# Decoder layer on one core: batch 0's keys and values projected in the turn before, x1's transposes earlier, and another spread of the first turn's score blocks

## The reference, cut to what matters

```
# 1: a lookup: the 8 best of 8192 keys for each token, and their values
h      = scan(h @ A + x @ Bm);  importance = softmax(x . (h @ W_imp.T))
shared = sum over n of neuron_w[b, n] * compress[n]            # a 256 x 128 matrix for each batch
scores = (x @ shared) @ K.T / sqrt(128)                        # 256 x 8192 for each batch
x1     = layernorm(x + sum of softmax(top8(scores)) * V[top8 index])
# 2: cross attention, 16 heads of 64, keys and values from the context
q = x1 @ Wq;  k, v = split(ctx @ Wkv)
attn   = softmax(clip(mask(q k / 8), -5, 5))
x2     = layernorm(x1 + (attn v) @ Wo + bo)
# 3: each expert set picks one token of each group of 32
x3     = layernorm(x2 + permuted feed-forward(x2))
```

## Time and profile before

| | before |
|---|---|
| median of 3 runs | 1438.27 us |
| lowest, highest | 1435.86, 1443.63 us |
| the profiled execution | 1435.45 us, its span 1433.4 us |
| busy over the span | PE 92%, PEld 69%, DVE 76%, ACT 50%, POOL 50% |
| mean granted TensorE clock | 0.964 of full speed |

### The profile page before, as it was taken

The page is one execution under the profiler, slowest core; times in us unless marked ns, Lnnn a source line. Parts: engine busy times, 40 slices in busy tenths (PEclk is TensorE's granted clock), DMA queues, the critical chain, the costliest instruction groups (busy, mean ns, idle before and its releaser), DMA issues.

```text
span 1433.4 us, 25145 instructions
## 1 busy us (share of the span) xinstructions
PE 1320.5 (92%) x9781; PEld 993.1 (69%) x9781; DVE 1087.0 (76%) x1625; ACT 723.9 (50%) x1361; POOL 723.2 (50%) x1010
## 2 busy tenths in 40 slices
PE   9765799999999999999999999999999969568998
PEld 5453577777878686868686878777777747346765
DVE  1369999888888888897978888888888841147567
ACT  1353465556464646465655555555556433135455
POOL 0524455556565646574746574655556573330225
PEclk7877899999999999999999999999999999889999
DMA  9451212121212222221213131212121210162323
GB/s 373 161 175 48 66 45 71 52 71 53 71 53 74 64 70 65 63 71 56 81 43 93 46 84 48 75 52 71 41 72 41 70 53 23 30 225 83 105 68 126
DMA packets 63174, 115.88 MB, mean 81 GB/s; under 512 B 9936, under 2 KB 43728, under 8 KB 61904
## 3 DMA queue, kind: packets, MB, share of 16 engines
q1 hardware_dynamic: 45968, 67.68, 15.6%
q0 software_dynamic: 14848, 41.96, 10.0%
q10 hardware_dynamic: 2240, 4.63, 0.9%
HBM read 103.49 MB, written 10.75 MB: 80 GB/s over the span
## 4 chain that ended last, share of the span: by engine, by line
PE 82%; DVE 9%; issue 3%; POOL 2%; DMA 2%; ACT 1%; SPq 0%; POOLq 0%; DVEq 0%; ACTq 0%
PE proj_bank L369 39%; PE score_bank L369 30%; PE sim_bank L369 10%; DVE cand_val L1048 2%; DVE cand_idx L1049 2%; PE score_bank L705 2%; DVE x_sum L1072 2%; POOL exp L1277 1%; POOL v_rows L1248 1%; DMA sc_in<-shared_compress 1%; PE sim_bank L705 1%; DVE dispatchedT L1187 1%; PE sim_bank L639 1%; DMA x_pair<-x_scratch 0%; PE sim_bank L520 0%
## 5 line engine op out<-in xcount | busy, mean ns | idle before, releaser
L811 ACT COPY score_row<-score_bank 128x512 f32<-128x512 f32 x512 | 298.6, 588 | 173.9 <-PE score_bank L369 102.2
L1048 DVE MAX8 cand_val<-score_row 128x8 f32<-128x2048 f32 x128 | 292.2, 2283 | 105.1 <-ACT score_row L811 105.1
L1248 POOL DMA_INDIRECT v_rows<-in_V,top_idx x256 | 248.2, 969 | 188.2 <-DVE top_idx L1062 106.3
L1277 POOL TENSOR_SCALAR exp<-exp,exp_bound 128x256 f32<-128x256 f32 x512 | 241.8, 488 | 107.0 <-ACT exp L823 106.3
L1049 DVE FIND_INDEX8 cand_idx<-cand_val,score_row 128x8 uint32<-128x2048 f32 x128 | 292.5, 2285 | 0.0
L369 PE MATMUL score_bank<-keysT_hi,qT_hi 128*128 128x512 f32 x512 | 219.1, 428 | 31.0 <-ACT score_row L811 30.0
L369 PE MATMUL score_bank<-keysT_lo,qT_hi 128*128 128x512 f32 x512 | 205.3, 401 | 0.0
L369 PE MATMUL score_bank<-keysT_hi,qT_lo 128*128 128x512 f32 x512 | 205.0, 400 | 0.0
L823 ACT ACTIVATE exp<-sim_bank 128x512 f32<-128x512 f32 x256 | 139.0, 595 | 91.8 <-PE sim_bank L369 91.8
L369 PE MATMUL sim_bank<-qT_heads,kT 64*128 64x256 f32 x1024 | 145.2, 402 | 7.7 <-ACT exp L823 7.7
L369 PEld LDWEIGHTS score_bank<-keysT_hi,qT_hi 128*128 128x128 f32 x512 | 98.2, 192 | 69.8 <-ACT score_row L811 34.9
(11 more groups left out here) (184 smaller groups left out, 2258.7 us busy)
## 6 DMA issues: line engine op xcount, KB each, us to landing
kT<-den_scratch SPq DMA_DIRECT2D x64, 256.0 KB, 4.0
x_pair<-x_scratch SPq DMA_DIRECT2D x32, 256.0 KB, 2.8
f_quads<-in_f POOLq DMA_DIRECT2D x32, 256.0 KB, 5.8
comp_then_wqkv_raw<-in_comp SPq DMA_DIRECT2D x6, 1024.0 KB, 18.3
xT_by_step<-in_xTs SPq DMA_DIRECT2D x4, 1024.0 KB, 9.1
keysT_raw<-in_KmT ACTq DMA_DIRECT2D x8, 512.0 KB, 12.7
xT_in<-in_xT SPq DMA_DIRECT2D x16, 256.0 KB, 3.8
x_sum<-in_x SPq DMA_DIRECT2D x32, 128.0 KB, 2.1
```

The source lines that it names most:

```text
L811: nc.scalar.copy(srow[n // PER % 2][:, i * CB:(i + 1) * CB], scb[n % 3]).then_inc(sem("score_evac"), 1)
L1048: own(nc.vector.max(cv[:, tile, cs], srow[g % 2][:, :]))
L1248: pool.indirect_dma_start(out=vg[:, k, :], out_offset=None, in_=V_rows, in_offset=bass.IndirectOffsetOnAxis(ap=i8[:, tile, k:k + 1], axis=0))\
L1277: last = nc.gpsimd.tensor_scalar(ex[i % NEX][:, k, :], ex[i % NEX][:, k, :], ub[:, k, c:c + 1], E_LO, ALU.min, ALU.max)
```

## The change

In turn -1 the keys and the values of batch 0 (`K` 0 to 3, then `V` 0 to 3) are projected two at a time at the end of each couple, behind its four blocks; before, the values stood beside b28 to b31 of that turn, and the keys beside b0 to b3 of turn 0. ACT's copies move with them. The rounding of the context of batch 0 to `ctx_hi` goes to the head of turn -1 on ACT; its counterpart `ctx_lo` on POOL stays where it was.

The transposes of batch 0's x1 (PE), their copies `x1T_hi` (ACT) and `x1T_lo` (DVE) go ahead of the last row of turn -1.

In turn 0 the blocks are spread anew by a function `blocks(c)`, which gives how many stand in the first part, beside the queries, in each couple and beside the values. Turn 0 has none in the first part, one beside each query job, six in each couple, one beside each value job; all other turns are as before. `den_inverse(0, 0)` goes from behind row 4 to ahead of row 3, and the weights of tile 1 of batch 1 (`weights8`) on ACT go behind couple 1.

```diff
+        def blocks(c):
+            if c == 0:
+                return [0, 0], [1, 1, 1, 1], [6, 6, 6, 6], [1, 1, 1, 1]
+            return [4, 4], [1, 1, 1, 1], [4, 4, 4, 4], [1, 1, 1, 1]
...
@@ PE
                 for j in range(4):
-                    if cross:
+                    if cross and c > 0:
                         project(("K", c, j), 1, 2 * j * P, cth, ctl)
-                    score(c, j)
+                    if early[0]:
+                        score(c, next(place))
...
-                    for e in range(4):
-                        score(c, 12 + 4 * j + e)
+                    for _ in range(couple[j]):
+                        score(c, next(place))
+                    if c == -1:
+                        need(pe, "ctx_lo", 1)
+                        need(pe, "w_lo", len(WCHUNKS))
+                        for i in (2 * j, 2 * j + 1):
+                            if i < 4:
+                                project(("K", 0, i), 1, 2 * i * P, cth, ctl)
+                            else:
+                                project_value(0, i - 4)
                 if cross:
                     values(c, NP // 2 - 1)
                     denominators(c, 1)
-                if mid:
+                if c == -1:
+                    x1_transpose(0, 0)
+                    x1_transpose(0, 1)
+                if mid and m:
                     need(pe, "ctx_lo", m + 1)
...
@@ DVE
+                if c == 0:
+                    den_inverse(c, 0)
                 candidates(c, 3)
...
                 candidates(c, 4)
-                if cross:
+                if cross and c > 0:
                     den_inverse(c, 0)
...
+                if c == -1:
+                    x1_lo(0, 0)
+                    x1_lo(0, 1)
                 candidates(c, 6)
                 candidates(c, 7)
-                if mid:
+                if mid and m:
                     x1_lo(m, 0)
                     x1_lo(m, 1)
```

More of the change, by code:

```diff
@@ L71, in turn_jobs @@
         jobs += [("q", c + 3, 0)]
+    if c == -1:
+        jobs += [("K", 0, j) for j in range(4)]
     if cross:
@@ L574, in _ @@
                 cross, mid, prep, out = (0 <= b < B for b in (c, m, a + 1, p))
+                early, query, couple, value = blocks(c)
+                place = iter(range(2 * SCORES))
                 if cross:
@@ L590, in _ @@
                         last.then_inc(full(key), 1)
-                    score(c, 4 + 2 * tile)
-                    score(c, 5 + 2 * tile)
+                    for _ in range(early[1] // 2):
+                        score(c, next(place))
                 if cross:
@@ L599, in _ @@
                         project(("Q", c, j), 0, 2 * j * P, x1h, x1l)
-                    score(c, 8 + j)
+                    for _ in range(query[j]):
+                        score(c, next(place))
                 if prep:
@@ L615, in _ @@
                     denominators(c, 1)
-                if mid:
+                if c == -1:
+                    x1_transpose(0, 0)
+                    x1_transpose(0, 1)
+                if mid and m:
                     need(pe, "ctx_lo", m + 1)
-                    need(pe, "w_lo", len(WCHUNKS))
                 for j in range(4):
-                    if mid:
[L621 to L629, removed]
+                    if mid and m:
+                        project_value(m, j)
+                    for _ in range(value[j]):
+                        score(c, next(place))
+                if mid and m:
                     x1_transpose(m, 0)
@@ L832, in _ @@
                 cross, mid, prep = (0 <= b < B for b in (c, m, a + 1))
+                early, query, couple, value = blocks(c)
+                place = iter(range(2 * SCORES))
+                if c == -1:
+                    context_hi(0)
                 for j in range(4):
-                    if cross:
+                    if cross and c > 0:
                         need(act, "ot_done", 2 * (c - 1) + 1 + j // 2)
                         heads_out(("K", c, j), kt[:, 2 * j:2 * j + 2, :].rearrange("p a s -> p (a s)"))
-                    score_out(c, j)
-                for e in range(4, 8):
-                    score_out(c, e)
+                    if early[0]:
+                        score_out(c, next(place))
+                for _ in range(early[1]):
+                    score_out(c, next(place))
                 for j in range(4):
@@ L844, in _ @@
                         heads_out(("Q", c, j), qt[:, 2 * j:2 * j + 2, :].rearrange("p a s -> p (a s)"))
-                    score_out(c, 8 + j)
-                    if mid and j == 1:
+                    for _ in range(query[j]):
+                        score_out(c, next(place))
+                    if mid and c and j == 1:
                         weights8(m, 1)
@@ L857, in _ @@
                         exps(c, 2 * j + 1)
-                    for e in range(4):
-                        score_out(c, 12 + 4 * j + e)
+                    for _ in range(couple[j]):
+                        score_out(c, next(place))
+                    if c == -1:
+                        for i in (2 * j, 2 * j + 1):
+                            if i < 4:
+                                heads_out(("K", 0, i), kt[:, 2 * i:2 * i + 2, :].rearrange("p a s -> p (a s)"))
+                            else:
+                                value_out(0, i - 4)
                     if c == -2 and j < 3:
```

38 lines of the change are left out of this document (29 added, 9 removed).

## The result

The changed kernel took 1458.79 us (median of four runs, 1453.89 to 1459.24) against 1438.17 us for the kernel before in the same comparison. The ratio is 1.0129, with a 95% interval of 1.0106 to 1.0151. The profiled execution took 1458.98 us, its span is 1456.9 us, 23.5 us over the one before. Of all the executions behind this document one, of a kernel in experiment 8, fell in a slow state (3175.62 us) and is left out of its ratio.

The account below looks back on a forecast made before the run. From turn 1 on PE sets the pace, so the time PE ends turn 0 decides. +2.5 + 9.8 + 2.5 = +14.8 us on the profiled 1435.45 gives 1450.2; forecast 1451 us, 8 in 10 range 1440 to 1457.

Parts of the forecast that it names:

- wrong in size: Sign: size is wrong if less than 38 or more than 46 us lie between the first `values` and turn 1.
- What bounds the kernel: From turn 1 PE sets the pace at 68.5 us a turn; any shift of turn 1's start moves the end equally.
- Turn -1: Key jobs wait some 5.7 us for `ctx_lo`, then run at half clock; DVE starts turn 0 2.5 us later.
- Up to the first values: In turn 0 PE arrives near 192 and waits for POOL's clips until about 207.4, through with first `values` at 208.5.
- Behind the first values: Rest of turn 0 takes 42.6 us against 32.8 before: +9.8, of which 4.3 are six blocks and 5.5 waits.
- 5.5 of waits: Waits between PE and DVE in turn 0 behind the first `values`, 5.5 of the +9.8 us.
- 2.5 for the clock: After PE's long wait ahead of the first `values`, work at half speed costs 2.5 us, between 0 and 3.1.
- the one behind the value sum of tile 1: Late turn 0: row 4 4.6 us, copies of b24 and b27 1.3, last `values` and denominators 3.7, V jobs and transposes 8.9.
- only the six blocks count: Second rival: the chain's waits are hidden and only order counts; +2.4 to +6.8 us, 1438 to 1445, chance 0.18.
- Faster: Third rival: PE finds the clips done at the first `values`; down to -8 us, 1430 us, chance 0.06.
- The fourth, more lost: Rival: second clock fall at the wait for row 6, or norm at 4.7 us; +19 to +23, 1455 to 1461, chance 0.09.
- the port as a loss: DVE's norm, sharing a port with POOL, takes 0.4 us if POOL's clips are through; otherwise the sum is 4.3 higher.

Follow-up runs that it names:

- experiment 8: Changed kernel with POOL's turn 0 order changed, then also `ctx_lo` of batch 0 early, then also the first reciprocal behind row 3: 1.0021, 0.9996, 0.9964 of the kernel before.
- the other trace of the changed kernel: The changed kernel measured once more with nothing altered: 1.0133 of the kernel before.
- experiment 5: Changed kernel with POOL making `ctx_lo` of batch 0 ahead of its gathers in turn -1: 1.0108 of the kernel before.
- experiment 6: Changed kernel with turn 0's old block spread, the reciprocal back behind row 4, and `ctx_lo` of batch 0 ahead of POOL's gathers: 0.9983 of the kernel before.
- experiment 4: Changed kernel with POOL making tile 1's inverse deviation behind the last head instead of head 9 in turn 0: 1.0120 of the kernel before.
- experiment 3: Changed kernel with POOL clipping heads 0 to 3 ahead of the gathers in turn 0: 1.0099 of the kernel before.
- last version of experiment 8: Changed kernel with POOL's turn 0 order changed, `ctx_lo` of batch 0 early and the first reciprocal behind row 3: 1437.02 us against 1441.69, ratio 0.9964.

## Why the prediction was right, and where its size was off

The forecast was 1451 us, with 1440 to 1457 for 8 in 10. The median of 1458.79 us lies 1.8 us above that; the ratio, applied to the 1438.27 us that the forecast started from, gives 1456.8, just inside. The prediction called itself wrong in size if less than 38 or more than 46 us lay between the first `values` and turn 1; there were 51.4, so by this sign its size was wrong. What follows goes through its steps.

**What bounds the kernel.** Right. The shift at PE's start of turn 1 is 263.10 - 238.76 = 24.3 us, and the span grew by 23.5. Of these, 2.3 us lie ahead of the changed part and are a difference between two executions; 22.0 us are the change's in this trace, and 18.5 in the other trace of the changed kernel, which is nearer to the ratio.

**Turn -1.** Right step by step. The first key job waits 5.60 us for `ctx_lo` (forecast 5.7) and runs at 0.50. DVE waits 1.14 us for row 4 (forecast 1.4) and 3.1 us in two pieces for the transposes (3.1). The start of turn 0 on DVE is 2.6 us later, forecast 2.5. That this cost goes away with an early `ctx_lo` is what experiments 5, 6 and 8 add.

**Up to the first values.** Right: PE came to them at 196.06 (forecast near 192, 2.3 us of the difference being the later trace) and waited 10.85 and 0.91 us for clips behind gathers behind `merge`. The point came 25.8 us after D where it was 24.9 before; the 0.9 us are the second half of `values` at half clock.

**Behind the first values.** Here the size was off. The forecast was 37.1 us of work, 5.5 of waits and 2.5 for the clock, 45.1 in all. Measured were 51.4 us in one execution of the changed kernel and 48.6 in the other (the stretch of the other, columns as in rows 1):

```profile
211.37:259.92 48.55, 39.65 (x248) 26.90 (x247) 34.22 (x41) 22.79 (x44) 23.23 (x36) 0.92 0.21 54
```

PE is idle for 8.9 us in both. So the term that was too small in both is the waits, 8.9 us where the sum had 5.5. The rest differs between the executions: PE is busy for 42.5 us at a mean clock of 0.86 in the one, 39.7 us at 0.92 in the other. Against 37.1 us of work that is, as an estimate, 5.4 and 2.6 us for the clock.

The step that failed is the one behind the value sum of tile 1: the forecast took DVE's row 4 (4.6 us) and the wait for row 6 (1.3 us) as what ends last there. In POOL's list, however, `rstd1(1, 1)` stands between heads 9 and 10. I had named POOL's order up to `ctx_lo` and not looked at what follows, though the same kind of reading (what stands ahead of the clips, and what does it wait for) had given the first wait. So the second half of the third `values` came at 242.0, after the value sum had ended at 239.5, and that half, one `sims`, six blocks, the last `values`, the denominators and the V jobs, 21.1 us, were still to do behind it, 3.9 us of them at half clock. From the end of the value sum to T the forecast had 4.6 + 1.3 + 3.7 + 8.9 = 18.5 us; measured were 23.7. Experiment 4 took the wait for the clips away and got the wait for row 6 that the forecast had there; in time it could not be told from the changed kernel.

**The rivals.** That only the six blocks count (+2.4 to +6.8) is refuted by the 8.9 us that PE is idle behind the first `values`. Faster is refuted at its own point. The fourth, more lost (+19 to +23, 1455 to 1461 us, chance 0.09), is the one whose size came, where the main forecast had 1445 to 1456. Of its two causes a half clock behind a second long wait did come, 0.50 behind 7.05 us, but the wait was for the clips of heads 10 and 11 and not for row 6; the norm on DVE took 0.4 us, as in the sum, so nothing here bears out the port as a loss.

**What was not foreseen in the experiments.** That the wait ahead of the first `values` would be worth 15 us by itself (experiment 3) was a mistake of the same kind as taking one row of the waits for a gain: with it gone the next waits in the ring take most of it back. Only when POOL's clips, gathers and inverse deviation (and `ctx_lo` of batch 1) were moved together did 0.011 come back. I can't say how the 0.011 divides between its parts beyond what experiments 3 and 4 show.

## What to carry to other kernels

Work that is moved off a busy stage is only worth something if the stage's next fixed point lies behind it. Look for the instruction that the stage can't pass, and read the whole in-order list of the engine that releases it, to its end, not to the first wait found. Where three engines wait for each other in a ring, a reordering is tried with all its lists at once: the same new spread was 1.3% slower than the kernel before with POOL's old order, 0.2% slower with the new order alone, and 0.4% faster once `ctx_lo` and the reciprocal had been moved too.

## What the runs showed of the hardware

I had counted half clock only behind long pauses. It can follow a wait of 2 us, and need not. The first stretch is the second `values` of the last version of experiment 8, behind its wait of 2.21 us; the second is the same job in the trace of experiment 4, behind a wait of 1.86 us:

```profile
201.88:205.30 3.42, 3.42 (x20) 1.78 (x24) 3.38 (x3) 0.00 (x0) 2.64 (x3) 0.56 0.29 81
```
```profile
217.86:219.81 1.95, 1.95 (x20) 1.13 (x24) 0.00 (x0) 0.00 (x0) 0.69 (x2) 1.00 0.03 8
```

At 0.56 it takes 1.5 us longer. The two executions of the changed kernel show the same with nothing else different: the first stretch is behind a wait of 1.87 us, the second behind one of 1.86.

```profile
221.98:225.14 3.16, 3.16 (x16) 1.53 (x16) 0.00 (x0) 0.00 (x0) 0.69 (x2) 0.58 0.02 5
```
```profile
220.39:222.26 1.87, 1.87 (x16) 1.06 (x16) 0.00 (x0) 0.00 (x0) 0.69 (x2) 1.00 0.04 9
```

These two executions differ by 3.5 us between q and T, and 2.8 of them lie behind the first `values`, where PE is idle for 8.9 us in both and only the clock differs (0.86 and 0.92). What decides between the two cases no run here shows. A difference of a few us between single traces of this program is therefore no finding; the ratios over several executions are.
